# Two attentions with 8 columns a head: a new order of the work in each slot

## The reference, cut to what matters

```python
    x = x + _L0_xattn_ref(_layernorm(x, axis=-1), ctx_512, ctx_512, L0_xattn_Wq, ...)
    ...
    x = x + _L3_xattn_ref(_layernorm(x, axis=-1), ctx_512, L3_xattn_Wq, L3_xattn_Wkv, L3_xattn_Wo)

        attn = jnp.einsum('bqhd,bkhd->bhqk', Q, K) * SCALE
        attn = jax.nn.softmax(attn, axis=-1)
        O = jnp.einsum('bhqk,bkhd->bqhd', attn, V).reshape(B, xN, DIM)
        return O @ Wo.T
```

## Time and profile before

| | us |
|---|---|
| median of three runs | 1390.44 |
| the profiled execution | 1382.45 |
| its span | 1380.7 |
| slots of L0x, from the scores in slot 2 (43.8) to the end of the stage (166) | 122 |
| slots of L3x, from the scores in slot 2 (1148.3) to the end of the stage (1280) | 132 |

### The profile page before, as it was taken

The page is one execution under the profiler, slowest core; times in us unless marked ns, Lnnn a source line. Parts: engine busy times, 40 slices in busy tenths (PEclk is TensorE's granted clock), DMA queues, the critical chain, the costliest instruction groups (busy, mean ns, idle before and its releaser), DMA issues.

```text
span 1380.7 us, 37780 instructions
## 1 busy us (share of the span) xinstructions
PE 1019.2 (74%) x15068; PEld 757.8 (55%) x15068; DVE 899.1 (65%) x2420; ACT 727.2 (53%) x1479; POOL 611.2 (44%) x575
## 2 busy tenths in 40 slices
PE   3788478889898565788977578978379675776774
PEld 2455366556677343356764356756267553555664
DVE  4677454788777995888975577866344266766432
ACT  5776355776555434555436456666155364664321
POOL 2566633354354432454551355642611345657132
PEclk9788588999999776788978779989589785887787
DMA  3321321110010101100001000000221112110122
GB/s 95 92 84 43 92 58 53 61 33 25 17 34 10 37 17 35 36 3 10 4 3 38 1 2 3 4 2 4 89 75 34 51 34 67 40 31 28 55 74 69
DMA packets 59721, 53.24 MB, mean 39 GB/s; under 512 B 10590, under 2 KB 47966, under 8 KB 59358
## 3 DMA queue, kind: packets, MB, share of 16 engines
q1 hardware_dynamic: 53777, 41.62, 10.4%
q0 software_dynamic: 4096, 8.40, 2.0%
q10 hardware_dynamic: 1679, 0.81, 0.2%
HBM read 33.90 MB, written 16.25 MB: 36 GB/s over the span
## 4 chain that ended last, share of the span: by engine, by line
PE 35%; issue 27%; DVE 23%; ACT 8%; POOL 3%; DMA 2%; POOLq 0%; ACTq 0%; SPq 0%; DVEq 0%
PE psum L671 12%; PE psum L1174 7%; PE psum L1192 6%; DVE area L1831 4%; PE psum L794 2%; PE psum L834 2%; DVE stats L1812 2%; ACT area L1261 2%; DVE area L1974 1%; DVE area L1988 1%; ACT xn L1285 1%; POOL sorted_in L2746 1%; DVE negm L1967 1%; DVE area L2127 1%; PE psum L678 1%
## 5 line engine op out<-in xcount | busy, mean ns | idle before, releaser
L1261 ACT ACTIVATE area<-psum 128x512 bf16<-128x512 f32 (+4 forms) x278 | 144.8, 540 | 206.1 <-PE psum L834 133.4
L1831 DVE TENSOR_TENSOR area<-psum,area 128x512 bf16<-128x512 f32 (+3 forms) x270 | 159.7, 620 | 50.4 <-ACT area L1261 46.8
L2472 DVE TENSOR_TENSOR area<-area 128x512 bf16<-128x512 f32 x106 | 73.4, 695 | 146.3 <-ACT area L1729 93.4
L2616 POOL TENSOR_TENSOR area<-area 77x1024 bf16<-77x1024 f32 x64 | 120.0, 1891 | 73.6 <-ACT area L1435 73.6
L1192 PE MATMUL psum<-moe,area 128*128 x1272 | 111.1, 229 | 24.2 <-issue 23.3
L1174 PE MATMUL psum<-xT_hi,moe 128*128 128x128 bf16 x848 | 115.5, 238 | 17.0 <-issue 13.7
L2572 POOL TENSOR_TENSOR moe<-stage,moe 128x512 bf16<-128x512 f32 x47 | 54.9, 1168 | 126.0 <-ACT moe L1256 126.0
L1435 ACT ACTIVATE area<-psum 77x1024 f32<-77x1024 f32 (+1 forms) x96 | 92.8, 1017 | 28.9 <-PE psum L794 28.9
L1192 PEld LDWEIGHTS psum<-moe,area 128*128 128x128 bf16 x1272 | 86.7, 102 | 37.5 <-issue 27.7
L2624 POOL TENSOR_SCALAR_AFFINE_SELECT area<-area 128x1024 bf16<-128x1024 bf16 x64 | 72.3, 1149 | 68.4 <-DVE area L1974 57.4
L1174 PE MATMUL psum<-xT_lo,moe 128*128 128x128 bf16 x424 | 95.3, 237 | 8.6 <-issue 8.5
(11 more groups left out here) (246 smaller groups left out, 3009.0 us busy)
## 6 DMA issues: line engine op xcount, KB each, us to landing
area<-sorted_in SPq DMA_DIRECT2D x22, 256.0 KB, 3.6
sorted_out<-area SPq DMA_DIRECT2D x22, 256.0 KB
stage<-in_w_L0m SPq DMA_DIRECT2D x16, 256.0 KB
stage<-in_w_L2m SPq DMA_DIRECT2D x16, 256.0 KB
stage<-in_w_L3m SPq DMA_DIRECT2D x16, 256.0 KB
sorted_in<-area SPq DMA_DIRECT2D x2, 1472.0 KB, 7.3
stage<-in_w_L2a SPq DMA_DIRECT2D x8, 320.0 KB
stage<-in_w_L1x SPq DMA_DIRECT2D x6, 320.0 KB
```

Source lines behind the costliest of these rows:

```text
L1261: ins = act.activation(out, bank, ACT.Copy)
L1831: ins = dve.tensor_tensor(out, bank, high, ALU.subtract)
L2472: dve.tensor_tensor(R.HL[u], R.HF[u], upper(R.HF[u]), ALU.subtract).then_inc(K.tile_split, tiles.one())
L2616: pool.tensor_tensor(A.PL[n % 4][0:A.L], A.PF[n % 4][0:A.L, :].rearrange("p (h q) -> p h q", h=8), A.PH[n % 4][0:A.L], ALU.subtract).then_ ...
```

## The change

In `dense`, on PE, DVE and ACT: `turn_outputs(b-4)` becomes the first step of a slot, and on PE and DVE `out_project(b-4)` moves from the end of the slot to a place ahead of `outputs(b-3)`; on PE and ACT `turn_maxima(b-1)` moves up. The moments of the next group are made at the end of the slot before (b % 4 == 3) instead of at the start of b % 4 == 0, and for L0x those of group 1 ahead of the prologue; the shift moves from behind the keys' low half to the slot's start. The last keys' values move from slots b % 4 == 0 to slots b % 4 == 1. On POOL the 1/deviation goes behind the exponentials and the last keys' values. `finished` makes the routed layer take on groups 0 and 1 one slot later (9, 10, 11 and 13, 14, 15 instead of 8, 9, 10 and 12, 13, 14); group 2 stays at 16, 17, 18.

```diff
@@ Dense.finished
-        g, rest = divmod(b - 2 * GB - slots, GB)
-        return g if g >= 0 and rest == 0 else None
+        for g in range(NG - 1):
+            if b == GB * (g + 2) + (g + 2 < NG) + slots:
+                return g
+        return None
@@ PE
+            if b >= 4:
+                turn_outputs(b - 4)
             if 0 <= b - 2 < B:
                 key_scores(b - 2)
             if b < B:
                 row_maxima(b, (0, 1))
+            if 0 <= b - 1 < B:
+                turn_maxima(b - 1)
             if ahead < NG and b % GB == 3:
                 queries_rows(ahead, (0, 1))
+            if b >= 4:
+                out_project(b - 4)
             if 0 <= b - 3 < B:
                 outputs(b - 3)
-            if b >= 4:
-                turn_outputs(b - 4)
-            if 0 <= b - 1 < B:
-                turn_maxima(b - 1)
...
-            if b >= 4:
-                out_project(b - 4)
@@ ACT
+            if b >= 4:
+                turn_outputs(b - 4)
             if 0 <= b - 2 < B:
                 exponentials(b - 2, 0)
                 exponentials(b - 2, 1)
+            if 0 <= b - 1 < B:
+                turn_maxima(b - 1)
...
-            if b < B and b % GB == 0:
-                late_values_hi(b // GB)
-            if b >= 4:
-                turn_outputs(b - 4)
-            if 0 <= b - 1 < B:
-                turn_maxima(b - 1)
...
+            if b < B and b % GB == 1:
+                late_values_hi(b // GB)
             g = A.finished(b, 0)
             if g is not None:
                 tokens_normed(A.then, g)
@@ DVE
+        if A.begun == 1:
+            g_stats(1)
...
-            if A.begun <= ahead < NG and b % GB == 0:
-                g_stats(ahead)
...
+            if ahead < NG and b % GB == 0:
+                shift_of(ahead, number[ahead])
+            if b >= 4:
+                turn_outputs(b - 4)
             if b < B:
                 row_maxima(b, (0, 1))
+            if b >= 4:
+                out_project(b - 4)
             if 0 <= b - 3 < B:
                 outputs(b - 3)
-            if b >= 4:
-                turn_outputs(b - 4)
...
                 if b % GB == 0:
                     keys_lo(ahead)
-                    shift_of(ahead, number[ahead])
...
                     values(ahead)
+                    if ahead + 1 < NG:
+                        g_stats(ahead + 1)
...
-            if b >= 4:
-                out_project(b - 4)
@@ POOL
+        if A.begun == 1:
+            rstd(slice(0, 128), group(1))
...
-            if A.begun <= ahead < NG and b % GB == 0:
-                rstd(slice(0, 128), group(ahead))
-            done = A.finished(b, 0)
-            if done is not None:
-                rstd(slice(0, 128), group(done))
-            if b < B and b % GB == 0:
-                late_values_lo(b // GB)
...
                 exponentials_lo(b - 2, 0)
                 exponentials_lo(b - 2, 1)
+            if b < B and b % GB == 1:
+                late_values_lo(b // GB)
+            if b % GB == 3 and ahead + 1 < NG:
+                rstd(slice(0, 128), group(ahead + 1))
+            done = A.finished(b, 0)
+            if done is not None:
+                rstd(slice(0, 128), group(done))
```

## The result

The change makes the kernel **slower: ratio 1.0285, 95% interval [1.0253, 1.0317]** (median 1425.39 us of four runs against 1391.35; the two medians alone divide to 1.0245, the two profiled executions to 1.0284). The forecast was 1399 us, with a range of 1381 to 1413: too low, and outside its range. Its sum was +8.7 us on the profiled execution; between the two profiled executions it is +39.3 us of span (1380.7 to 1420.0).

A forecast was written before the change was run, and what follows sets the result against it. No engine is full; the engine-to-engine chain inside a slot and queue order set the time. L0x +3.7 and L3x +5.0 give +8.7 us on the 1390.44 median: 1399 us, range 1381 to 1413.

The forecast's parts named there:

- late chain: Slots 4, 8, 10, 14: engines wait in turn before PE may project; +3.0, +1.1 and +4.55 us in slots 4, 8, 10.
- stuck shift: Slots 4 and 8: DVE's shift meets a POOL split of weights and takes 1.15 us instead of mostly 0.16.
- The chain in slot 10: Slot 10: last keys, 1/deviation, shift, finished tokens and turned outputs wait in turn, 6.6 us, before PE projects; slot +4.55 us.
- the forecast 3.0 us: Slot 11 of L0x: group 0's routing leaves, where PE had waited 2.86 us for DVE; -3.0 us.
- The rule that was weighed: Slots 4 and 8: DVE and POOL lock a shared port, first starter keeps it; DVE first: 4 us lower, 1 in 10.
- the forecast's own row: Shift at 143.68 us: POOL began first by 0.07 us and the shift took 1.21 us, so 1.15 was kept.
- -1.55, -1.75, +0.75: L0x: slots 5 and 9 shorten by 1.55 and 1.75 us; slots 6 and 7 together lengthen by 0.75.
- the first rival: Both stages: the new order pays because stalls lie beside other work; 1369 us at best, half gives 1380; chance 0.23.
- what stands behind the projection: Slots 4, 8, 10, 14: PE's work after projecting, such as outputs and row maxima; some 2.85 us in slot 10.
- the stage's end: L0x from slot 16: POOL may do exponentials' low halves ahead of 1/deviation while DVE sorts; -2.7 us.
- stays as long: Start of L3x: POOL's work against the additions keeps its length; gain costed at nothing, bounds -4.5 and +1 us.
- The rival that named the slower side (1413): Slots of both stages: idle stretches lower PE's clock too, costing about 12 to 18 us; 1413 us; chance 0.25.

The follow-up runs named there:

- e17: The whole change with one POOL edit: the finished group's 1/deviation is back at the slot's head, ahead of exponentials and last keys' values; ratio 1.0198.
- e1: Kernel before with the new order alone: outputs turned first, maxima turned earlier, projection ahead of outputs; other parts as before; ratio 1.0178.
- e9: Kernel before with only the outputs turned first, on PE, ACT and DVE; maxima and projection in their old places; ratio 0.9983.
- e5: Kernel before with outputs turned first and maxima turned earlier, but the projection at the slot's end on PE and DVE; ratio 1.0136.
- e6: Kernel before with the new order alone, but the projection directly behind the outputs on PE and DVE; ratio 1.0137.
- e2: The whole change with the next group's shift alone put back behind the keys' low half; ratio 1.0246.
- e4: The whole change with the last keys' values put back in slots b % 4 == 0 and their old queue places on ACT and POOL; ratio 1.0118.
- e13: Kernel before with outputs turned first and projection at the slot's end; ACT turns maxima early, PE turns them behind the outputs; ratio 1.0084.

## Why the prediction was wrong, point by point

**Right: what each late chain does.** Slots 4 and 8: DVE's wait 1.48 (1.45 forecast), stuck shift 1.11 (1.15), PE let go. The slot grew by 4.2 where 3.0 was forecast, slot 8 by 2.8 (1.1). The chain in slot 10 is there with all its links; +6.7 us (4.55 forecast). Slot 11 gave back the forecast 3.0 us. The rule that was weighed, the Trainium skill's, SBUF — State Buffer, section "SBUF: two separate sides", agrees with three rows: whoever was first kept the other out, POOL by 0.07 us in the forecast's own row, by 0.05 in slot 4 of the change and by 0.04 in e17. That DVE could be first and pass in 0.16 us, by which the sum would have been 4 us lower, did not happen in any of these rows, nor in slot 8 or in L3x, where the shifts took 1.11, 1.12 and 1.11 us; in slot 10 the shift took 0.16 us with no operation of POOL beside it.

**Wrong: the step in which the new order itself cost nothing.** The forecast took the order as a list of single stalls, and gave slots that have neither a late chain nor routing next to nothing or a gain: -1.55, -1.75, +0.75, and in the first rival even 10.7 us a stage of gain. e1 has no late chain, and costs 13.2 us in L0x and 1.78% in all (some 24 us), more than the whole forecast of +8.7. The place is the slack between two queues: before, ACT and DVE had until the slot's end to copy and split the turned outputs; now PE, in each slot, waits until both have ended all work of the slot before, then copied, then split, and only then does outputs. I had counted "what stands behind the projection" in slots 4, 8, 10 and 14 only. The price was missed by a factor and not by a detail: in e1 PE waits for the low halves 13 times in L0x's slots, before 6 times. e9 against e5 and e1 shows that the early turn of the outputs is not it (0.9983), and that the projection (data) or the outputs' bank (with the maxima turned early) are.

**Wrong: the four banks were read and not used.** `take` tells that each result waits for the fourth before it; the forecast never laid the new order of results beside it. In the change the projection is the fourth after the turned outputs, and reads them as well; in e5 and e6 the outputs are the fourth, and read nothing of them. In e9, where the outputs are the third, there is no loss.

**Missed: slot 3, +3.9 us.** With the late values in slot 1, POOL's work lies without a gap beside DVE's four masks. e1, e2 and e4 have slot 3 at 7.3 to 7.6 us, and e2 keeps the late values where the change has them: a collision in time, not a cost of the work. Before, the first mask had begun 0.09 us ahead of a low half of POOL's and took its 0.47 us, and it was POOL's operation that took 1.51 us instead of 1.25.

**Mis-sized: slots 12 to 14 and 16.** +7.2 us in the first three where +2.8 was forecast, and slot 16 takes 3.2 us more where the stage's end was to give back 2.7; it gave that back later (3.0 from slot 17 on). In L3x, for which the forecast took the same, the end cost 2.5 us more, and why is open. Slots 12 and 16 wait for the turned outputs behind routing and sorting on DVE (PE for 3.69 and 4.74 us). L3x went as L0x, +5.0 forecast, 18.2 measured; its slot 2 took 2.5 us more (13.44 against 10.92), where the forecast had bounded it at +1: one of the additions took 6.51 us, 5.35 before. The forecast held that POOL's work there "stays as long"; but the low half of the last keys' values (L2678, 1.13 us) now stands in it, and the addition lasts until POOL's run of operations is over. That is 1.2 of the 2.5 us.

**The rival that named the slower side (1413) had the direction and the wrong cause.** It put 12 to 18 us on PE's clock. The granted clock did fall, from 0.86 to 0.77 over L0x's slots and from 0.77 to 0.76 over L3x's, and groups such as 0.78 against 0.50 us are there. But PE's busy time in the slots grew by 4.9 + 0.9 = 5.8 us in all, with the same instructions, and with the weight loads taken in (PE or PEld busy) it is the same 5.8 us. That bounds what the slower clock cost PE itself, out of 43.1. The other 37.3 us are PE's idle time: waits made the loss, and the clock fell with them.

**Also short: sums of parts.** The late values cost 0.4% alone and 1.7% in the change; the finished groups gain 0.2% alone, which its interval doesn't tell from nothing, and cost 0.6% in the change. e17 shows one of these meetings: POOL's order put the late values between the moments and the 1/deviation that the next slot's first step hung on.

What stays open: how e5's 1.36% divides between the bank and the place of the maxima on ACT, since e13 takes the one wait away and brings another of 18.1 us; and how much of the late values' 1.7% is slot 3's collision and how much the chain, since e4 takes away both.

## What to carry to other kernels

Where queues are in order and meet each slot, ask of each moved step not only what it waits for, but how much time lay between its producer's end and its use, and whether the step behind it in the queue has any other reason to wait: a use that moves from a slot's end up behind its producer turns a slot of slack into none, in every slot (the projection in e1), while the producer can move to the head at no cost (e9). With rotating buffers, write the new order of takes down and look at the n-th before each: a consumer may wait for data it never reads. And try parts alone as well as in company; here sooner moments and later finished groups, which stood inside a loss of 2.85%, are a gain of 0.6% once the shift, the late values and the order are left alone.

## What the runs showed of the hardware that was not expected

- Masks that read one tensor each (96 x 1024 or 96 x 256, bf16, and a column of factors) are held up beside POOL, not only operations with two: 5.18 us for four, where eight take 3.5 us in all in the same stretch of e4 (2.26 and 1.26).
- A single addition of 128 x 128 on DVE (L2367), 0.35 us by its median, took up to 6.5 us beside POOL after, and 5.35 before. It ended as a run of POOL's element-wise operations did, five of them after and four before: it did not get in between two of them.
- The collision depends on some tenths of a microsecond: slot 3 is 11.4 us in the change and 7.6 in e2, which moves nothing but the shift and has one POOL operation 0.6 us later.
